# Merge of a transformer block rebuilt: first batch made ready during attention, gate folded into the output weights, rows normalised on ScalarE

## What is computed

```python
mod = (silu(c) @ wmod).reshape(2, 6, 1, 256)     # sa, ca, ga, sb, cb, gb
ga = (2 * (ga >= 0) - 1) * maximum(abs(ga), 0.25)   # gb likewise
h = layernorm(x) * (1 + ca) + sa
x = x + ga * attention(h)      # 16 heads of width 16, q, k, v, o with low-rank adapters
h = layernorm(x) * (1 + cb) + sb
x = x + gb * (shared_swiglu(h) + routed_swiglu(h))  # routed: top 1 of 8 experts
```

## Time and profile before

| what | value |
|---|---|
| median of 3 runs | 1949.0 us (1946.54 to 1949.53) |
| the profiled execution's own time | 1948.8 us |
| its span, first to last instruction | 1946.8 us |
| mean granted TensorE clock | 0.98 of full speed |
| TensorE / VectorE / ScalarE / GpSimd busy | 1866.7 / 1561.0 / 1244.7 / 342.8 us |
| moved by DMA | 141.52 MB, mean 73 GB/s |

### The profile page before, as it was taken

One profiled execution on the slowest core, in us unless ns is written; L12 is line 12 of the kernel. 1 busy time (PEld: TensorE's weight loads), 2 busy tenths in 40 slices (PEclk: granted clock), 3 DMA queues, 4 the chain that ended last, 5 costly groups with the idle time before them and its releaser, 6 DMA issues.

```text
span 1946.8 us, 34638 instructions
## 1 busy us (share of the span) xinstructions
PE 1866.7 (96%) x13114; PEld 768.0 (39%) x13115; DVE 1561.0 (80%) x2738; ACT 1244.7 (64%) x1423; POOL 342.8 (18%) x425
## 2 busy tenths in 40 slices
PE   8898999999999999999999999999976899999997
PEld 5442222222222222222222222222225655599996
DVE  6678999999999999999999999999717632245553
ACT  5446777777777777777777777777861221144442
POOL 5464100000000000000000000000016532223333
PEclk9998999999999999999999999999997799999998
DMA  5332111111111111111111111111056433322221
GB/s 189 131 123 77 52 61 49 43 39 57 57 49 42 40 57 57 49 42 39 59 57 48 42 40 55 55 45 39 9 176 224 139 109 99 109 85 69 73 73 49
DMA packets 87961, 141.52 MB, mean 73 GB/s; under 512 B 11200, under 2 KB 58304, under 8 KB 87824
## 3 DMA queue, kind: packets, MB, share of 16 engines
q1 hardware_dynamic: 72424, 101.61, 16.1%
q0 software_dynamic: 10240, 32.40, 5.0%
q10 hardware_dynamic: 5160, 5.64, 0.8%
HBM read 90.84 MB, written 48.51 MB: 72 GB/s over the span
## 4 chain that ended last, share of the span: by engine, by line
PE 83%; DVE 9%; DMA 3%; ACT 2%; SPq 1%; issue 1%; POOL 1%; POOLq 0%; DVEq 0%; ACTq 0%
PE ps L1002 24%; PE ps L991 20%; PE ps L968 15%; PE ps L1661 7%; DVE mx L1047 6%; PE ps L1212 5%; PE ps L1684 3%; PE ps L1546 3%; PE ps L626 2%; DMA l_in<-inverse_sums 1%; ACT prob L1080 1%; PE ps L643 1%; DMA qk_parts<-parts 1%; DVE x L1298 1%; PE ps L975 0%
## 5 line engine op out<-in xcount | busy, mean ns | idle before, releaser
L1047 DVE TENSOR_REDUCE mx<-ps 128x1 f32<-128x512 f32 x2048 | 1275.4, 684 | 39.7 <-PE ps L968 35.8
L1080 ACT ACTIVATE prob<-ps 128x1024 f32<-128x1024 f32 x1024 | 992.4, 1021 | 274.7 <-PE ps L991 272.2
L1002 PE MATMUL ps<-prob,vs 128*32 128x512 f32 x4096 | 546.3, 605 | 0.7 <-ACT prob L1080 0.7
L968 PE MATMUL ps<-k_high,q_high 64*128 64x512 bf16 x2048 | 400.4, 387 | 3.4 <-DVE mx L1047 3.3
L991 PE MATMUL ps<-q_high,k_high 64*128 64x512 bf16 x2048 | 390.0, 377 | 2.9 <-ACT prob L1080 1.8
L991 PE MATMUL ps<-q_low,k_low 34*128 34x512 bf16 x2048 | 390.4, 378 | 0.0
L968 PEld LDWEIGHTS ps<-k_high,q_high 64*128 64x128 bf16 x2048 | 99.0, 92 | 645.8 <-DVE mx L1047 624.7
L1108 POOL CAST mb<-turned_sb 16x128 bf16<-16x128 f32 x32 | 9.0, 281 | 916.1 <-ACT turned_sb L1069 892.2
L991 PEld LDWEIGHTS ps<-q_low,k_low 34*128 34x128 bf16 x2048 | 100.0, 94 | 117.3 <-issue 0.5
L991 PEld LDWEIGHTS ps<-q_high,k_high 64*128 64x128 bf16 x2048 | 101.3, 96 | 88.4 <-ACT prob L1080 29.4
L1002 PEld LDWEIGHTS ps<-prob,vs 128*32 128x32 f32 x4096 | 80.6, 108 | 118.6 <-issue 113.3
(11 more groups left out here) (150 smaller groups left out, 1413.4 us busy)
## 6 DMA issues: line engine op xcount, KB each, us to landing
k_high<-qk_parts SPq DMA_DIRECT2D x126, 128.0 KB
qk_parts<-parts SPq DMA_DIRECT2D x32, 384.0 KB, 3.1
k_low<-qk_parts SPq DMA_DIRECT2D x128, 64.0 KB
head_out<-head_out_sb SPq DMA_DIRECT2D x32, 256.0 KB, 10.8
q_high<-qk_parts SPq DMA_DIRECT2D x126, 64.0 KB
sorted_in<-zero_row POOLq DMA_DIRECT2D x13, 390.0 KB, 7.0
xs<-sorted_in SPq DMA_DIRECT2D x39, 130.0 KB
q_low<-qk_parts SPq DMA_DIRECT2D x64, 64.0 KB
```

The lines of the kernel that those rows point to most:

```text
L968: pe.matmul(ps[:, ring.bank((n, m, u)), :], q_high[p][mine, t * P:(t + 1) * P], k_high[p][mine, c * CH:(c + 1) * CH], start=True, stop=Tru ...
L1002: mm = pe.matmul(ps[32 * j:32 * j + 32, 7, :], vs[buf(h)][:, kt, :], prob[:, kt % 2, j * CH:(j + 1) * CH], start=(kt == 0), stop=(kt == KT ...
L1047: dve.tensor_reduce(mx[n % 2][:, at, c:c + 1], ps[:, ring.bank(what), :], AX.X, ALU.max).then_inc(s_ring, 1)
L1080: act.activation(prob[:, kt % 2, :].rearrange("p (u c n) -> p u c n", u=2, c=2)[:, :, half, :], ps[:, 2 * half:2 * half + 2, :], ACT.Exp). ...
```

## The change

In DRAM, h2_rows and x1_rows are laid out as (chunk, partition, row, 256), so that one partition's part of a chunk is one piece of 4 KB; token rows are read from it row by row.

During attention, in SP's new `prepare(n)`, called at the end of `turn` of head n:

```diff
+                prepare(num(h))
+            def prepare(n):
+                if n == X_AT:
+                    for c in range(CPB):
+                        sp.dma_start(xg[c][:], rows(io["x"], (CPB + c) * TPC, TPC)).then_inc(s_xin, 16)
+                if n == XB_AT:
+                    sp.wait_ge(s_xb, CPB)
+                    for c in range(CPB):
+                        sp.dma_start(xg_dram[c], xg[c][:]).then_inc(s_xgst, 16)
+                if n == XB_AT + 1:
+                    sp.wait_ge(s_xgst, 16 * CPB)
+                    for c in range(CPB):
+                        sp.dma_start(xg[c][:], rows(io["x"], c * TPC, TPC)).then_inc(s_xin, 16)
+                if n == FIRST_AT:
                     fetch_sums(sp, 0)
+                if n == FIRST_AT + 1:
+                    sp.wait_ge(s_vs, H)
+                    for c in range(CPB):
+                        for k in range(HALF):
+                            load_heads(sp, o_first[c], c, 0, k, s_oin)
+                if n == FIRST_AT + 2:
                     store_inverse(sp, 0)
+                if n == FIRST_AT + 3:
+                    sp.wait_ge(s_rlst, 32)
+                    for c in range(CPB):
+                        for k in range(HALF):
+                            load_inverse(sp, c, 0, k, s_oin)
+                if n == NEXT_AT:
+                    fetch_sums(sp, 1)
+                if n == NEXT_AT + 2:
+                    store_inverse(sp, 1)
+                    for c in range(CPB):
+                        load_heads(sp, o_in[c], c, 1, 0, s_oin)
+                if n == NEXT_AT + 3:
+                    sp.wait_ge(s_rlst, 64)
+                    sp.wait_ge(s_on, CPB)
+                    for c in range(CPB):
+                        load_inverse(sp, c, 1, 0, s_oin)
...
-            merge_load(sp, 0, 0, 0, 0)
-            merge_load_x(sp, 0, 0)
-            merge_load(sp, 1, 1, 0, 1)
+            for c in range(CPB):
+                sp.dma_start(xg[CPB + c][:], xg_dram[c]).then_inc(s_xg, 16)
```

Before the last head store SP loads the biased x of chunks 4 to 7 back. On VectorE `invert(dve, 0)` and `invert(dve, 1)` stand behind the first pair of heads 20 and 27. GpSimd scales the output weights once for each batch, adds the bias to x and multiplies the heads:

```diff
+                    if m == 0 and n == FIRST_AT + 3:
+                        invert(dve, 0)
+                    if m == 0 and n == NEXT_AT + 3:
+                        invert(dve, 1)
             negate(dve, NH - 1)
-            invert(dve, 0)
...
+            def bias(turn, b):
+                pool.wait_ge(s_xin, 16 * CPB * (turn + 1))
+                for c in range(CPB):
+                    hold(pool)
+                    pool.tensor_tensor(xg[c][:], xg[c][:], gbo[:, bass.ds(b, 1), :].to_broadcast([P, TPC, D]),
+                                       ALU.add).then_inc(s_xb, 1)
...
-                    pool.dma_start(dst[:, bass.ds(i, 1)], io[name][:, bass.ds(i, 1)]).then_inc(s_expert, 16)
-                elif i < E:
+                if i < E and u == 0:
+                    pool.dma_start(rgT[:, bass.ds(i, 1)], io["rgT"][:, bass.ds(i, 1)]).then_inc(s_expert, 16)
+                elif i < E and u == 2:
...
+            pool.wait_ge(s_weff, 2)
+            for b in reversed(range(B)):
+                pool.tensor_tensor((woT, woT1)[b][:], woT[:], rowmod[:, b, 0, :].unsqueeze(1).to_broadcast(
+                    [P, HALF, D]), ALU.mult).then_inc(s_wo, 1)
+                pool.wait_ge(s_wo, B - b)
             for n in range(2, NH):
                 if n + 1 < NH:
                     following(n)
+                if n == X_AT + 2:
+                    bias(0, 1)
+                if n == XB_AT + 3:
+                    bias(1, 0)
+                if n == FIRST_AT + 6:
+                    pool.wait_ge(s_oin, 16 * 4 * CPB)
+                    for c in range(CPB):
+                        hold(pool)
+                        pool.tensor_tensor(o_first[c][:], o_first[c][:], l_in[c][:], ALU.mult).then_inc(s_on, 1)
+                if n == NEXT_AT + 6:
+                    pool.wait_ge(s_oin, 16 * 6 * CPB)
+                    for c in range(CPB):
+                        hold(pool)
+                        pool.tensor_tensor(o_in[c][:, 0, :], o_in[c][:, 0, :], l_in[c][:, 0, :],
+                                           ALU.mult).then_inc(s_on, 1)
                 split_maxima(pool, step, n)
-            pool.wait_ge(s_exp_free, AHEAD + 2 * KT * NH)
```

`following` no longer loads ruT, and GpSimd issues no rdT at attention's end. fetch_sums(2) covers heads 24 to 31. The merge is written out, chunk by chunk:

```diff
+            fetch_sums(sp, 2)
+            last_heads(0)
+            last_heads(1)
+            store_x1(0)
+            last_heads(2)
+            last_heads(3)
+            store_inverse(sp, 2)
+            store_x1(1)
+            sp.wait_ge(s_rlst, 96)
+            last_inverse(0)
+            last_inverse(1)
+            store_x1(2)
+            last_inverse(2)
+            last_inverse(3)
+            store_h2(0)
+            store_x1(3)
+            sp.dma_start(before[:], io["before"]).then_inc(s_before, 16)
+            for g in range(CPB, NCH):
+                store_h2(g - 3)
+                store_x1(g)
+            for g in range(NCH - 3, NCH):
+                store_h2(g)
+            sp.wait_ge(s_op, NCH)
+            merged(sp)
             for e in range(E):
+                sp.dma_start(ruT[:, e:e + 1], io["ruT"][:, e:e + 1]).then_inc(s_expert_late, 16)
+            for e in range(E):
+                sp.dma_start(rdT[:, e:e + 1], io["rdT"][:, e:e + 1]).then_inc(s_expert_late, 16)
+        def merged(eng):
+            eng.wait_ge(s_x1st, 16 * NCH)
+            for u in range(NH2):
+                eng.wait_ge(s_h2st[u], 16 * ((NCH - u + NH2 - 1) // NH2))
...
+            def out_proj(g):
+                o, w = (o_first[g], woT) if g < CPB else (o_in[g - CPB], woT1)
+                pe.wait_ge(s_on, min(g + 1, CPB) if g < CPB else 2 * CPB)
+                wait(pe, s_onlast, g - CPB + 1)
...
+            for g in range(CPB):
+                out_proj(g)
+            turn(0)
+            out_proj(4)
+            turn(1)
+            route_logits(0)
+            out_proj(5)
+            turn(2)
+            route_logits(1)
+            out_proj(6)
+            turn(3)
+            route_logits(2)
+            out_proj(7)
+            turn(4)
+            route_logits(3)
             pe.wait_ge(s_shared, 48)
             pe.sem_inc(s_gu_free, AHEAD)
+            pe.wait_ge(s_x1, NCH - 1)
+            gate_up(pe, 0, 0)
+            turn(5)
+            route_logits(4)
+            turn(6)
+            route_logits(5)
+            turn(7)
+            route_logits(6)
+            route_logits(7)
             pe.wait_ge(s_x1, NCH)
             gate_up(pe, 0, 1)
...
+            def divide(c):
+                dve.wait_ge(s_olast[c], 32)
+                dve.tensor_tensor(o_in[c][:, 1, :], o_in[c][:, 1, :], l_in[c][:, 1, :],
+                                  ALU.mult).then_inc(s_onlast, 1)
+            def residual(g):
                 dve.wait_ge(s_op, g + 1)
+                dve.tensor_tensor(xg[g][:], ps[:, OUT_BANK[g % 2]:OUT_BANK[g % 2] + 2, :].rearrange(
+                                      "p c (t d) -> p (c t) d", d=D), xg[g][:], ALU.add).then_inc(s_x1, 1)
+            def moments2(g):
                 dve.wait_ge(s_x1, g + 1)
                 for t in range(TPC):
+                    st = dve.bn_stats(stats2[g % 2][:, t, :], xg[g][:, t, :])
                 step(st)
                 hold(dve)
                 for t in range(TPC):
+                    a = dve.bn_aggr(mv2[:, g, t, :], stats2[g % 2][:, t, :])
                 a.then_inc(s_var2, 1)
+            def factors(g):
                 dve.wait_ge(s_std2, g + 1)
+                step(dve.reciprocal(std2[:, g, :], std2[:, g, :]))
+                dve.scalar_tensor_tensor(shift2[:, g, :], mv2[:, g, :, 0], -1.0, std2[:, g, :], ALU.mult,
+                                         ALU.mult).then_inc(s_shift2, 1)
+            dve.wait_ge(s_xb, NCH)
+            dve.wait_ge(s_xg, 16 * CPB)
+            residual(0)
+            moments2(0)
+            invert(dve, 2)
+            factors(0)
+            for g in range(1, NCH):
+                residual(g)
+                if g == CPB - 1:
+                    divide(0)
+                moments2(g)
+                factors(g)
+                if CPB - 1 <= g < NCH - 2:
+                    divide(g - CPB + 2)
...
+            def normalize2(g):
+                act.wait_ge(s_shift2, g + 1)
+                wait(act, s_h2st[g % NH2], 16 * (g // NH2))
+                for t in range(TPC):
+                    a = act.activation(h2[g % NH2][:, t, :], xg[g][:, t, :], ACT.Identity,
+                                       bias=shift2[:, g, t:t + 1], scale=std2[:, g, t:t + 1])
+                a.then_inc(s_n2, 1)
...
+            for g in range(NCH):
+                if g >= 3:
+                    take(g - 3)
+                if g >= 4:
+                    take_logits(g - 4)
+                root2(g)
+                normalize2(g)
+            shared_silu(act, 0, 0)
+            for g in range(5, NCH):
+                take(g)
                 take_logits(g - 1)
             take_logits(NCH - 1)
+            shared_silu(act, 0, 1)
```

324 lines of the change are left out of this document (107 added, 217 removed).

## The result

| | before | after |
|---|---|---|
| median, beside each other on one chip (4 runs each) | 1947.77 us (1946.09 to 1949.53) | 1911.86 us (1910.39 to 1914.37) |
| ratio | | 0.982, 95% interval 0.9808 to 0.9832 |
| span of the profiled execution | 1946.8 us | 1910.1 us |
| mean granted TensorE clock | 0.98 | 0.986 |

The change saves 35.9 us by the medians, 36.7 by the spans. 43.3 were predicted, 1906 us; 1911.9 lies in the range. Projection g, turn g, logits g and factor g are the output projection, the transposes, the routing logits and VectorE's second factor instruction (L1419) of chunk g; the tail is what TensorE has between projection 7 and the end of logits 7. The first down product of the shared expert starts at a merge time of 134.7 before and 95.6 after.

The account below looks back on a forecast made before the run. VectorE leads attention; in the 111 us merge no engine is full and VectorE has little pause. Merge and routing -46.8, attention +3.5, together -43.3 from 1948.8: 1905.5, stated as 1906, range 1898 to 1922.

Parts of the forecast that it names:

- Attention, +3.5: Attention: two reciprocals of 1.75 us between VectorE's reduces cost +3.5 us (bounds 0 and 3.5); everything else there costs nothing.
- VectorE's chunk, 3.97: Merge, VectorE per chunk: residual 1.25, statistics to reciprocal 2.52, factors 0.2, together 3.97 us.
- Projection 4 to 7: Merge: TensorE sets a period of 6.6 us; projection 4 ends 1467.4, projection 7 ends 1487.2.
- The one slow projection that was allowed for: Merge: one output projection at TensorE's low clock, 5.40 instead of 3.67, allowed for with +1.7 us.
- The tail: Merge's end: TensorE's turns, logits and one gate and up pair behind projection 7 take 16.9 us at full clock.
- rival 1: Merge and shared products: TensorE's clock stays low, slowing projections, gate and up pairs and logits 7; +12, 1918; chance 0.14.
- Behind the merge: Logits 7 to rank products' end 7.5, routing 10.5: hidden product at 1524.3 against 1571.12; expert block loads cost 0.
- The clock: Same as rival 1: TensorE's clock stays low in the merge; +12, 1918; chance 0.14.
- The port: Merge: divisions and factors wait for GpSimd instructions (2.36 each) on VectorE's road; +13 at most, 1919, likelier 1912; chance 0.12.
- The table reloads: Merge: ScalarE reloads tables between square root and affine copy, 2 x 1.28 us a chunk; 1918; chance 0.03.
- The transfers: Shared stage: experts' 8.4 MB on SP's queue delay x1 and token rows, costing beyond 36 us; 1953; slower chance 0.03.
- the three that were to make the prediction wrong: Merge: projections over 8 us apart; second factor instruction over 2 us; shared stage: TensorE waiting for residuals.

Follow-up runs that it names:

- experiment 3: Changed kernel with both attention reciprocals, their stores, loads and GpSimd products moved behind VectorE's last reduce: 1917.01 us, ratio 0.9843.
- experiment 4: Changed kernel with the two reciprocals inside attention left out, all waits, stores and loads kept (output values differ): 1911.7 us in one run.
- experiment 11: Changed kernel with the edits of experiment 1, experiment 2 and experiment 5 together: 1904.51 us, ratio to before 0.9782.
- experiment 5: Changed kernel with each of attention's two reciprocals cut into eight pieces of 32 columns, one at every second pair of reduces: 1911.5 us, ratio 0.9818.
- experiment 6: Changed kernel with the second factor instruction (two SBUF operands, 128x4) written as four of 128x1 with one SBUF operand and two scalars: 1913.25 us, ratio 0.9829.
- experiment 8: Changed kernel with output weights unscaled; VectorE multiplies by the gate in its own instruction ahead of the residual: 1931.57 us in one run.
- experiment 7: Changed kernel with rows normalised by VectorE again instead of ScalarE, one subtract-and-multiply instruction per row: 1913.35 us in one run.
- experiment 10: Changed kernel with 32 more 512 KB blocks on SP's queue ahead of the ruT and rdT blocks: 1935.78 us in one run.
- experiment 9: Kernel before with only its eight rdT blocks moved, issued by GpSimd behind the merge instead of at attention's end: 1941.62 us in one run.
- experiment 1: Changed kernel with one gate and up pair moved from behind the last logits to before turn 6: 1908.13 us, ratio to before 0.9801.
- experiment 2: Changed kernel with four dead 128x512 products in TensorE's pause between turn 0 and projection 4: 1912.34 us, ratio 0.9822.

## Why the prediction was right, and where its sizes were off

The sign, the place and the mechanism held: the merge was shortened, the stages behind it did not move, and the hidden product (1, 0) ends at 1534.38 instead of 1571.12, 36.7 earlier, exactly the difference of the spans. Part of that number is luck: after's setup happened to be 2.1 us shorter in its profile. Without it the two profiles would lie 34.6 apart, 39.1 won in the merge less 4.4 lost in attention. Two slips of the prediction's sums don't matter: its low end adds up to 1899.3, not 1898, and the start of the third reciprocal to 1450.65, not 1450.4. By the steps:

- **Attention, +3.5.** The growth was 4.4, all of it the two reciprocals (experiments 3 and 4). The first cost 1.59, near the 1.75 put down; the second 3.07, since the products behind its pause ran on the low clock, some 1.4 us more. That SP's new transfers finish before the next head's was too sure: experiment 11 has one that TensorE waited for, 1.05 us. That VectorE leads was read rightly from the earlier trace rows; that any instruction there is paid in full was not: cut in pieces it costs half (experiment 5). In the profiled executions only 2.33 of it shows at the head copy, because of the shorter setup (first negated maximum at 132.58 against 134.68; between 131.65 and 134.95 over the kernels here, in its first loads).
- **VectorE's chunk, 3.97.** The residual took 1.23 (1.25 predicted), ScalarE's four rows 2.08 (1.9). The factor was the unclear term: 0.2 taken, 2.56 the upper bound. It was 0.16, 0.88 and 1.05 in chunks 0 to 2, so the first division ended at 1467.46, 1465.1 on before's clock, against 1463.7 predicted. The division itself took 1.72 (1.9). The inverses that it needs were to land some 5 us before it and landed just in time (experiment 6).
- **Projection 4 to 7.** TensorE does set the period: 6.11 us, not 6.6. The 3.67 + 1.05 + 1.85 were added up, though the rows overlap by some 0.17 each at the hand-overs. The one slow projection that was allowed for came (5.17). Projection 7 ended at 1491.09, 1488.8 on before's clock, against 1487.2.
- **The tail, the step that failed.** It was sized at full clock: 16.9 us from there to the end of logits 7, with 2.2 as allowance for all of the merge. It took 22.2. Three logits at 3.24 to 3.55 instead of 1.85 are 4.7, turn 7 another 0.9. Behind them the first gate and up pair took 6.1 instead of 3.43, 2.7 more. The argument "TensorE now has work nearly without a gap" spoke against rival 1 and was the wrong test: TensorE was busy nearly throughout and the granted clock fell all the same. The pause ahead of turn 6 was short by luck: factor 7 took 0.16, and where it took 1.72 turn 6 came 1.5 us later (experiment 4).
- **Behind the merge.** Ranks and routing took 21.1 from logits 7 to the hidden product; predicted 18.0, and the slow pair is 2.7 of the difference. The routing itself took 10.7 (10.5).

On before's clock that makes: +1.6 at projection 7, +3.1 more at logits 7, +3.1 more behind them, together 7.8 late; the head copy 1.2 earlier than the +3.5 said: 6.6, the whole miss (36.7 against 43.3).

**The rivals.** *The clock* came by two thirds: some 8 of its 12 us beyond what the forecast allowed. One projection of four was slow (1.5 of its 6.9 us) and one pair (2.7 of 4.8), but turn 7 and the last three logits took 5.6 more where it had counted 1.7. *The port* came true as a mechanism. Ahead of projection 4 it held factors 1 and 2 and the first division for 2.7 us, 1.4 more than the forecast had in it. L1419 took up to 2.24, but in chunks 4 to 6 that lies beside TensorE's 6.1; in chunk 7 it does not, as experiments 4 and 8 show. The Trainium skill ("SBUF — State Buffer", section "SBUF: two separate sides") gives this lock to VectorE instructions with two SBUF inputs, against a GpSimd instruction that reads SBUF, and to those in a two-port mode. By that rule the trace agrees: the 128x4 instruction with two SBUF tensors was held (up to 2.24) and the 128x1 ones of experiment 6 were not (0.58). The 128x256 ones with one SBUF tensor were held too, in experiment 7 (2.31 against 1.38) as in L1314 of the earlier trace rows, so the prediction's "two SBUF operands" is too narrow for what it read there. Whether those ran in a two-port mode no run shows. *The table reloads* did not come: one load at the start of the merge and none between square root and affine copy. *The transfers* of the experts' blocks did not cost anything, and experiment 10 puts the threshold at 40 us where 36 was forecast. Not seen as a term of its own was the move of rdT (experiment 9, 7.7 us). It was within the total, because the new first chunks were summed without it.

**Its own signs.** Of the three that were to make the prediction wrong, one came: L1419 took over 2 us, 2.24 in chunk 3 (at 1469.88). It cost nothing there, since TensorE's road was longer. The other two did not come: the projections lie 6.1 us apart, 7.6 from 4 to 5, and TensorE waits for no residual in the shared stage (once for a hidden product, 0.46). Logits 7 end 43.5 us earlier against the end of attention, where 48 were named. The clock near 1 held for projections 5 to 7, not for 4 and not in the tail.

## What to carry to other kernels

When several edits make a stage short, price the new stage twice, once at each level of TensorE's clock, and look at what kind of work TensorE has there, not only whether it has work: here some 8 us beyond the forecast hung on it, and putting a wide product pair among the turns and small products, with a few dead products in the one pause and the reciprocals in pieces, gave 7 us back. Before moving small work off a crowded stage into a long one, ask which engine leads the long one; there a long instruction costs its length and what the clock loses in the pause, and short pieces cost half; it can be worth that, as here, where late reciprocals won 4.4 us in attention and lost 9 in the merge. Count a wait on a queue by what stands behind it. And follow a small instruction that may be held by another engine to the last chunk too, where nothing longer hides it.

## What the runs showed of the hardware

The granted clock of after in 4 us windows (columns as above; the clock is the third number from the end of each row), at the pause ahead of projection 4 and in the tail:

```profile
1460.00:1464.00 4.00, 1.25 (x9) 0.86 (x8) 3.41 (x11) 2.18 (x5) 4.00 (x2) 0.97 0.37 128
1464.00:1468.00 4.00, 0.44 (x1) 0.47 (x2) 3.89 (x5) 3.03 (x6) 3.92 (x3) 0.50 0.84 290
1468.00:1472.00 4.00, 4.00 (x14) 3.28 (x14) 3.45 (x9) 0.30 (x1) 3.92 (x2) 0.68 0.71 280
...
1500.00:1504.00 4.00, 3.82 (x24) 3.85 (x25) 0.00 (x0) 1.20 (x4) 2.15 (x1) 0.66 0.26 104
1504.00:1508.00 4.00, 4.00 (x21) 4.00 (x21) 0.00 (x0) 1.26 (x3) 0.00 (x0) 0.50 0.54 168
1508.00:1512.00 4.00, 3.63 (x18) 3.57 (x18) 0.00 (x0) 0.19 (x1) 0.00 (x0) 0.50 1.04 424
```

In the 8 us from 1460 to 1468, where the clock first falls, TensorE was busy 1.7. Where it falls again TensorE had been busy nearly all the time, with turns and 128x8 logits, and the clock went to the lower of its two levels (1.2 GHz) all the same. By 1520 it was at 1.00 again. In experiment 1 logits 5 and 6, behind a gate and up pair, kept their full-clock lengths. What exactly the chip counts, the runs don't say.

Projection 4, always behind the same pause, took 5.17, 6.70, 6.66, 6.49, 6.67 and 5.67 in six executions (after and experiments 1, 6, 10, 5 and 4) whose merge up to there differs in the factors at most. How much of the low stretch falls on it is not fixed, and single executions differ by 1.5 us there for that reason alone.

A wait of 1.50 us, as TensorE had behind each of the two reciprocals in attention, was followed by the low clock behind the second and not behind the first. It is the same in all seven profiled executions of kernels with both reciprocals whole (after and experiments 1, 2, 6, 7, 8 and 10), and the second head grew by 3.07 to 3.13 us there, the first by 1.59. With the second in pieces or moved away the clock stayed up. What sets the two places apart is open.
